# Listing transfers of a batch without pace, and first projections on their own loads, in an attention and mixture-of-experts kernel

## Chip, cores and metric

The kernel runs on one core of a Trainium2 chip. The metric is the device time of one execution in microseconds (us). Engines are named as the profile does: PE (TensorE), ACT (ScalarE), DVE (VectorE), POOL (GpSimd) and SP (SyncE, which here only issues DMAs).

## What is computed

```python
def reference(x, Wq, bq, ..., router_w0, wg0, wu0, wd0, ...):   # x: 8 x 1024 x 256, 16 heads of 16
    x = layernorm(x + attention(x))        # rotary q, k; softmax(q k / 4) v; output projection
    x = layernorm(x + moe(x))
    return x

def moe(x2):                               # all 8192 tokens; two groups g of 32 experts
    scores = softmax(x2 @ router_w[g])
    weight, expert = top_k(scores, 2)
    # token rows sorted by expert, silu(xs @ wg) * (xs @ wu) @ wd, times weight, added back
```

## The kernel before, in words

The program has two phases, `attention_phase` and `expert_phase`. The change lies in the first. It runs one loop over steps t, from -56 to 597, written out for each engine. A batch b has 64 steps, 64b to 64b+63; a unit u is 4 of the 16 heads, 16 steps long. In a step t PE does four things, in order: score tiles of step t+26 (`score`, line 694, into `ps_a`; DVE takes the row maxima of them, line 939), the transposed scores of step t (`score_t`, line 684, into `ps_b`; ACT makes exponentials, line 570), the product with v of step t-2 (`pv`, line 712, 8 matmul records a step, into `ps_o`), and the jobs that `schedule` has put at t: Q and K (`features`, line 625, a quarter of a projection each), V (`values`, line 632), M (the maxima of a unit, transposed), O, T, L and R (output projection, transposed activations, router logits, counts). PE is in order: where one of these waits, the rest waits.

In this text "step n of batch b" is counted by `pv`: the stretch from the start of the product of loop step 64b+n to the next. PE issues that product in loop step 64b+n+2, so what the code puts at loop step 33 falls in step 31 of this count.

Every engine is in order, and each has its own list. SP takes the list `turns`, sorted by step and then by a priority number; each transfer in it is preceded by its waits, and SP stands at them. POOL takes `pool_order`, sorted by step. What bears on the change:

- Heads' projections of a batch's half c go through `split`: ACT writes the features (line 540), SP swaps their halves by DMA (`swap`, line 339), POOL rotates (lines 238, 239, 241; DVE does so for the very first half), DVE masks an upper part (line 259), POOL subtracts (line 249), SP writes both parts out (`parts_out`, line 344), and SP loads them as stacks for a unit (`stack`, line 362, 8 DMAs, priority 1). `score` waits for the stack of its unit. For the first unit of batch b+1 the stack stands at turn 64b+33 and is needed from loop step 64b+38 on; `parts_out` stands at +29 and +30, `swap` of the second half at +49 and +51.
- Listing: each token row of the attention's result is written to the rows of its chosen experts. For tile t (0 to 7) of batch b, SP loads the rows into one of two buffers (`stage_in`, line 440, priority 7, turn 64(b+2) + 27 + 4(t - 1.5), after a wait until the tile before in the same buffer has been written); POOL marks them (line 518) and issues four indirect DMAs (`scatter_rows`, line 106), each after a wait until `pv` has reached 64(b+2) + 26 + 4t + n. So the 32 transfers of batch b go one a step, in loop steps 27 to 58 of batch b+2. Batches 0 to 5 are listed beside attention work (of batches 2 to 7), batch 6 after the last step, batch 7 in the expert phase.
- `split_max` (lines 778, 781) is a chore of DVE at loop step 16u - 10, thus in steps 4, 20, 36 and 52 or just after; `split_upper` (line 259) comes 8 and 11 steps after `k_step`, which is -48 and -16 from the batch's start. `top2` (lines 815 to 824) has DVE do 48 short instructions from loop step 64(b+1)+55 on. `bias_y` is POOL's at +57.
- Start: SP issues the load of x (`s_xt`) and nine parameter loads (`s_par`). PE waits for four memsets of POOL (the ones, line 485, is the last) and for DVE's constants before anything; `features` of batch 0 waits for all nine loads too, as ACT does. V of batch 0 stands at steps -7 to 0, the second Q and K at -24 to -17.

Of the kernel before, what the change touches and what calls it, by code (L numbers as in the profile page):

```python
# [17 lines left out]
SPB = UPB * STEPS  # L18
# [35 lines left out]
def schedule(nb):  # L54
# [3 lines left out]
    for b in range(nb):  # L58
# [3 lines left out]
        for c, at in enumerate((start - 56, start - 24)):  # L62
            for q in range(QUARTERS):
                put(b_jobs, at + q, "Q", b, c, q)
                put(b_jobs, at + QUARTERS + q, "K", b, c, q)
        for i in range(KC):
            put(b_jobs, start - 7 + i, "V", b, i)
# [11 lines left out]
SPILL = 3 * P  # L79
LISTS = NG * TOPK  # L80
# [28 lines left out]
def attention_phase(nc, nb, dram, keep, cols):  # L109
# [25 lines left out]
    with ExitStack() as ctx:  # L135
# [67 lines left out]
        s_list = keep["s_list"]  # L203
        block = ctx.enter_context(nc.Block())
# [6 lines left out]
        k_step = lambda b, c: SPB * b + (-48, -16)[c]  # L211
        pool_order = []
        for b in range(nb):
# [6 lines left out]
            if b < nb - 1:  # L220
                for t in range(KC):
                    pool_order.append((SPB * (b + 2) + 27 + 4 * t, "list", (b, t)))
# [101 lines left out]
        def _(sp):  # L324
            sp.dma_start(x_t[:, :, :], dram["x_t"][0]).then_inc(s_xt, 16)
            for dst, src in ((w_q, "w_q"), (bias, "bias"), (w_k, "w_k"), (consts, "consts"), (trig, "trig"), (w_v, "w_v"),
                             (w_o, "w_o"), (bo_row, "bo_row"), (router, "router")):
# [19 lines left out]
            def stack(u):  # L347
# [6 lines left out]
                sp.wait_ge(s_ones, 2 * NSTK)  # L354
# [91 lines left out]
            for b in range(nb):  # L446
# [13 lines left out]
                if b + 1 < nb:  # L460
                    turns.append((SPB * b + 3, 6, next_x, (b + 1,)))
                    for t in range(KC):
                        turns.append((SPB * (b + 2) + 27 + LISTS * (t - 1.5), 7, stage_in, (b, t)))
# [11 lines left out]
        def _(pool):  # L475

            for i in range(NSTK):
                for n, lo in enumerate((SIDE // 2, SIDE + SIDE // 2)):
                    pool.memset(k_stack[i][lo:lo + SIDE // 2, :, :], -1.0).then_inc(s_ones, 1)
            pool.wait_ge(s_ones, 2 * NSTK)  # L480
            pool.memset(v_sb[0][:, :], 1.0).then_inc(s_ones, 1)
# [7 lines left out]
            pool.wait_ge(s_par, 16 * 9)  # L489
            for _, name, args in pool_order:  # L490
# [19 lines left out]
                elif name == "list":  # L510
# [9 lines left out]
                    for n, (g, kk) in enumerate((g, kk) for g in range(NG) for kk in range(TOPK)):  # L520
                        pool.wait_ge(s_pv, min(SPB * (b + 2) + 26 + LISTS * t + n, n_steps))
# [4 lines left out]
        def _(act):  # L526
# [7 lines left out]
            def features(which, b, c, q):  # L534
                src = arrived()
                if (b, c) == (0, 0):
                    act.wait_ge(s_par, 16 * 9)
# [5 lines left out]
            def values(b, i):  # L543
                src = arrived()
                if b >= 2:
                    act.wait_ge(s_pv, SPB * (b - 1))
                act.activation(v_sb[b % 2][:, i * H * VW:(i + 1) * H * VW].rearrange("p (h d) -> p h d", d=VW)[:, :, 0:DH],
# [53 lines left out]
        def _(pe):  # L601
# [16 lines left out]
            def features(which, b, c, q):  # L618
                out = b_tile()
                if b == 0:  # L620
                    pe.wait_ge(s_par, 16 * 9)
                pe.wait_ge(s_xt, 16 * (b + 1))
# [6 lines left out]
            def values(b, i):  # L629
                out = b_tile()  # L630
                for dc in range(DC):
# [84 lines left out]
            pe.wait_ge(s_ones, 2 * NSTK + 3)  # L716
            pe.wait_ge(s_set, NSET)
            for t in range(first, steps_end):
                ta = t + LEAD
# [29 lines left out]
        def _(vec):  # L749
# [165 lines left out]
            vec.wait_ge(s_par, 16 * 9)  # L915
# [656 lines left out]
```

## Time and profile before

| what | value |
|---|---|
| median of 3 runs | 2739.4 us (2738.84 to 2759.41) |
| the profiled execution's own time | 2749.05 us |
| its span, first to last instruction | 2747.2 us |
| granted TensorE clock, mean over the span | 0.907 |
| first `score` | at 58.5 us |
| first `score_t` (step 0) | at 127.2 us |
| last product with v | at 1845 us |
| expert phase | from 1959.6 us |

All durations come from the profiled execution. A window A:B is in us from its first instruction. In a window restricted to line 712, 8 records (x8) are one step, so a stretch of 24 records is three steps; its length against that of the same steps of another batch tells what was lost in it.

### The profile page before, as it was taken

The numbers are of one execution on the slowest core, as the hardware profiler recorded it, in microseconds if no ns is written. First come the engines' busy times: TensorE is split into PE (matmuls) and PEld (weight loads), VectorE is DVE, ScalarE is ACT, GpSimd is POOL, SyncE is SP. The second block draws the span as 40 slices with busy tenths as digits, with TensorE's granted clock in tenths as the row PEclk, the third lists the DMA queues.
The fourth block names the chain that finished last, engine by engine and source line by source line (L and its number), as shares of the span: only waits on it lengthen the run. The fifth ranks groups of instructions, "written<-read, shape, count | busy, mean of one in ns | idle before, by whom it ended". The sixth has DMA issues, their size and how long they took to land. (4 is left out here: it accounts for less than half of the span.)

```text
span 2747.2 us, 44206 instructions
## 1 busy us (share of the span) xinstructions
PE 2283.7 (83%) x12531; PEld 1149.5 (42%) x12531; DVE 1877.7 (68%) x3693; ACT 1526.6 (56%) x3206; POOL 1090.0 (40%) x963
## 2 busy tenths in 40 slices
PE   2999999999999999999999989983059998999900
PEld 1433333433433433433433333322037776777700
DVE  2988878888779778788778879512315544666766
ACT  0277777767676766766767757750013333333344
POOL 2221230343443444444335342325445554555543
PEclk7899999999999999999989989965579999999955
DMA  4423432533444444443543542223466645788782
GB/s 124 107 44 87 126 79 66 128 83 109 143 105 113 131 111 120 132 123 90 145 124 76 141 130 58 73 65 111 156 228 208 230 148 170 229 238 245 233 293 88
DMA packets 205593, 371.48 MB, mean 135 GB/s; under 512 B 31984, under 2 KB 145136, under 8 KB 201136
## 3 DMA queue, kind: packets, MB, share of 16 engines
q1 hardware_dynamic: 142864, 259.69, 34.7%
q0 software_dynamic: 27552, 75.40, 7.7%
q10 hardware_dynamic: 34944, 33.56, 4.1%
q8 instruction: 112, 1.84, 0.3%
q14 instruction: 121, 0.99, 0.1%
HBM read 206.62 MB, written 135.69 MB: 125 GB/s over the span
## 5 line engine op out<-in xcount | busy, mean ns | idle before, releaser
L939 DVE TENSOR_REDUCE maxima_sb<-ps_a 128x1 f32<-128x1024 f32 x1024 | 1227.1, 1219 | 311.8 <-PE ps_a L694 301.8
L570 ACT ACTIVATE probs_sb<-ps_b 128x512 f32<-128x512 f32 x2048 | 1093.6, 599 | 432.4 <-PE ps_b L684 425.3
L694 PE MATMUL ps_a<-k_stack_sb,q_stack_sb 48*128 48x512 f32 x2048 | 747.9, 457 | 110.9 <-DVE maxima_sb L939 66.6
L684 PE MATMUL ps_b<-q_stack_sb,k_stack_sb 50*128 50x512 f32 x2048 | 789.3, 466 | 12.7 <-issue 7.1
L694 PEld LDWEIGHTS ps_a<-k_stack_sb,q_stack_sb 48*128 48x128 f32 x2048 | 317.5, 192 | 712.3 <-DVE maxima_sb L939 379.6
L712 PE MATMUL ps_o<-probs_sb,v_sb_sb 128*32 128x512 f32 x4096 | 571.0, 631 | 12.7 <-ACT o_raw_sb L578 11.9
L1217 POOL DMA_INDIRECT y_dram<-y_rows_sb,spot_sb x318 | 304.9, 959 | 293.5 <-DVE y_rows_sb L1469 283.4
L684 PEld LDWEIGHTS ps_b<-q_stack_sb,k_stack_sb 50*128 50x128 f32 x2048 | 325.9, 190 | 111.2 <-ACT probs_sb L570 72.6
L1321 PE MATMUL ps_g<-w_gu_sb,x_cols_sb 128*128 x1272 | 357.5, 404 | 6.1 <-issue 2.9
L106 POOL DMA_INDIRECT rows_dram<-stage_sb,listed_sb x224 | 216.6, 967 | 335.9 <-PE ps_o L712 307.1
L1249 ACT ACTIVATE x_cols_sb<-ps_x 128x256 f32<-128x256 f32 x318 | 121.9, 383 | 255.9 <-issue 125.4
L1454 DVE TENSOR_TENSOR spot_sb<-x_rows_sb,spare_sb 128x1 int32<-128x1 int32 x318 | 50.7, 160 | 298.6 <-ACT gate_sb L1269 204.2
L1321 PEld LDWEIGHTS ps_g<-w_gu_sb,x_cols_sb 128*128 128x128 f32 x1272 | 219.2, 192 | 59.0 <-issue 29.6
L238 POOL TENSOR_TENSOR feat_qk_sb<-feat_qk_sb,trig_sb 128x1024 f32<-128x1024 f32 x30 | 71.2, 2374 | 354.9 <-DMA swapped_sb<-feat_qk_sb 267.2
L1269 ACT ACTIVATE gate_sb<-ps_g 128x128 f32<-128x128 f32 x318 | 88.2, 277 | 217.8 <-PE ps_g L1321 165.1
L1339 PE MATMUL ps_y<-w_d_sb,hidden_t_sb 128*128 x636 | 192.7, 385 | 0.0
L1310 PE MATMUL ps_x<-consts_sb,x_rows_sb 128*128 128x128 f32 x636 | 124.1, 278 | 62.8 <-DMA x_rows_sb<-rows_dram 62.8
L712 PEld LDWEIGHTS ps_o<-probs_sb,v_sb_sb 128*32 128x32 f32 x4096 | 83.0, 110 | 184.7 <-ACT probs_sb L570 62.9
L1469 DVE COPY y_rows_sb<-ps_y 128x256 f32<-128x256 f32 x318 | 132.0, 415 | 5.4 <-remote 3.1
L1310 PEld LDWEIGHTS ps_x<-consts_sb,x_rows_sb 128*128 128x128 f32 x636 | 90.3, 143 | 98.1 <-DMA x_rows_sb<-rows_dram 65.9
L540 ACT ACTIVATE feat_qk_sb<-ps_b,bias_sb 128x256 f32<-128x256 f32 x128 | 60.6, 474 | 86.6 <-PE ps_b L625 84.4
L1339 PEld LDWEIGHTS ps_y<-w_d_sb,hidden_t_sb 128*128 128x128 f32 x636 | 97.0, 193 | 25.1 <-issue 1.5
(158 smaller groups left out, 2071.2 us busy)
## 6 DMA issues: line engine op xcount, KB each, us to landing
x_rows_sb<-rows_dram SPq DMA_DIRECT2D x318, 128.5 KB
swapped_sb<-feat_qk_sb SPq DMA_DIRECT2D x64, 256.0 KB
parts_dram<-parts_q_sb SPq DMA_DIRECT2D x16, 1024.0 KB
parts_dram<-parts_k_sb SPq DMA_DIRECT2D x16, 1024.0 KB
q_stack_sb<-parts_dram SPq DMA_DIRECT2D x64, 256.0 KB
k_stack_sb<-parts_dram SPq DMA_DIRECT2D x64, 256.0 KB
w_gu_sb<-w_gu SPq DMA_DIRECT2D x8, 2048.0 KB, 20.2
back_sb<-y_dram ACTq DMA_DIRECT2D x64, 256.0 KB
```

Of the source, the lines that this page charges most:

```text
L106: return pool.indirect_dma_start(dram["rows"][g], bass.IndirectOffsetOnAxis(ap=index, axis=0), source, None)
L570: act.activation(probs[t % NPR][:, j, :], src[:, :], ACT.Exp, scale=float(DH) ** -0.5).then_inc(s_bdrain, 1)
L684: pe.matmul(out[:, :], k_stack[u % NSTK][lo:lo + XROWS, jj, kc * P:(kc + 1) * P].bitcast(F32R), q_stack[u % NSTK][lo:lo + XROWS, jj, qh * ...
L694: ins = pe.matmul(out[:, kh, :], q_stack[u % NSTK][lo:lo + ROWS, jj, qt * P:(qt + 1) * P].bitcast(F32R), k_stack[u % NSTK][lo:lo + ROWS, j ...
L712: ins = pe.matmul(ps_o[32 * j:32 * j + 32, :], v[:, at:at + 32], probs[t % NPR][:, j, :], start=kc == 0, stop=kc == KC - 1)
L939: vec.tensor_reduce(maxima[u % 2][:, 1 - k, i:i + 1], src[:, :, :].rearrange("p a q -> p (a q)"), AX.X, ALU.max).then_inc(s_adrain, 1)
L1217: pool.indirect_dma_start(dram["y"][n // NT], bass.IndirectOffsetOnAxis(ap=spot[n % NSP][:, :], axis=0), y_rows[n % NY][:, :], None).then_ ...
L1249: act.activation(x_cols[n % NXT][:, :, :], ps_x[n % 2][:, 0:DC, :], ACT.Copy).then_inc(s_xc, 1)
L1310: ins = pe.transpose(ps_x[n % 2][:, dc, :], x_rows[n % NXG][:, dc * P:(dc + 1) * P], con("ident"))
L1321: ins = pe.matmul(ps_g[n % 2][:, 0:2 * HID], x_cols[n % NXT][:, dc, :], w_gu[g][:, bass.ds(e * (DC * 2 * HID) + dc * 2 * HID, 2 * HID)], s ...
L1339: pe.matmul(ps_y[n % 2][:, 0:D], hidden_t[n % 2][:, :], w_d[:, bass.ds(e * D + down_at(g), D)], start=True, stop=True).then_inc(s_down, 1)
L1469: vec.tensor_copy(y_rows[m % NY][:, :], ps_y[m % 2][:, 0:D]).then_inc(s_yr, 1)
```

## The change

It makes four edits, all in `attention_phase` and `schedule`.

1. Listing: the first transfer of a batch waits until `pv` has done 64(b+2)+31 steps, the other 31 wait for no step. `pool_order` has tile t at +31+2t (before +27+4t), and `stage_in` stands at turn +31+2(t-1.5), which is 28, 30, 32, ... 42 (before 21, 25, 29, ... 49).
2. The loads of w_q, bias and w_k count on x's semaphore, and the first projections (PE and ACT) wait for those four loads only. The trigonometric table is loaded ahead of the constants. The other waits count six parameter loads.
3. POOL fills the first v buffer before the stacks' rows; PE waits for the memsets and DVE's constants only at step -26. V waits for its own.
4. For batch 0, V moves from steps -7 to 0 to steps -46 to -39, and the second Q and K from -24 to -36 (with them `k_step`, so the swap, the masks and `parts_out` of the half come 12 steps earlier).

```diff
-        for c, at in enumerate((start - 56, start - 24)):
+        for c, at in enumerate((start - 56, start - (36 if b == 0 else 24))):
...
-            put(b_jobs, start - 7 + i, "V", b, i)
+            put(b_jobs, start + i - (46 if b == 0 else 7), "V", b, i)
...
+LIST_AT, LIST_PACE = 31, 2
...
+        x_in = lambda b: 16 * (3 + b + 1)
...
-        k_step = lambda b, c: SPB * b + (-48, -16)[c]
+        k_step = lambda b, c: SPB * b - (48, 28 if b == 0 else 16)[c]
...
-                    pool_order.append((SPB * (b + 2) + 27 + 4 * t, "list", (b, t)))
+                    pool_order.append((SPB * (b + 2) + LIST_AT + LISTS // LIST_PACE * t, "list", (b, t)))
...
-            for dst, src in ((w_q, "w_q"), (bias, "bias"), (w_k, "w_k"), (consts, "consts"), (trig, "trig"), (w_v, "w_v"),
-                             (w_o, "w_o"), (bo_row, "bo_row"), (router, "router")):
+            for dst, src in ((w_q, "w_q"), (bias, "bias"), (w_k, "w_k")):
+                sp.dma_start(dst[:], dram[src][:]).then_inc(s_xt, 16)
+            for dst, src in ((trig, "trig"), (consts, "consts"), (w_v, "w_v"), (w_o, "w_o"), (bo_row, "bo_row"),
+                             (router, "router")):
...
-                        turns.append((SPB * (b + 2) + 27 + LISTS * (t - 1.5), 7, stage_in, (b, t)))
+                        turns.append((SPB * (b + 2) + LIST_AT + LISTS // LIST_PACE * (t - 1.5), 7, stage_in, (b, t)))
...
+            pool.memset(v_sb[0][:, :], 1.0).then_inc(s_ones, 1)
+            pool.wait_ge(s_ones, 1)
             for i in range(NSTK):
...
-                        pool.wait_ge(s_pv, min(SPB * (b + 2) + 26 + LISTS * t + n, n_steps))
+                        if t == n == 0:
+                            pool.wait_ge(s_pv, min(SPB * (b + 2) + LIST_AT, n_steps))
...
                 if (b, c) == (0, 0):
-                    act.wait_ge(s_par, 16 * 9)
+                    act.wait_ge(s_xt, x_in(0))
...
-                if b == 0:
-                    pe.wait_ge(s_par, 16 * 9)
-                pe.wait_ge(s_xt, 16 * (b + 1))
+                pe.wait_ge(s_xt, x_in(b))
...
-            pe.wait_ge(s_ones, 2 * NSTK + 3)
-            pe.wait_ge(s_set, NSET)
             for t in range(first, steps_end):
+                if t == -LEAD:
+                    pe.wait_ge(s_ones, 2 * NSTK + 3)
+                    pe.wait_ge(s_set, NSET)
```

## Rows read from the trace of the kernel before

**Rows 1.** The page's first part: busy time of the engines.

```profile
PE 2283.7 (83%) x12531; PEld 1149.5 (42%) x12531; DVE 1877.7 (68%) x3693; ACT 1526.6 (56%) x3206; POOL 1090.0 (40%) x963
```

**Rows 2.** Windows, line 712 alone: stretch, us, PE busy (x), clock, DMA. Batches 1, 2.

```profile
329.10:541.81 212.71, 70.45 (x512) 0.98 0.38 91
541.81:770.44 228.63, 72.53 (x512) 0.94 0.43 113
```

**Rows 3.** Windows, line 712: steps 60 to 62, batches 1, 2; sum of 1 to 6.

```profile
528.40:538.55 10.15, 3.19 (x24) 1.00 0.38 77
750.27:767.19 16.92, 4.07 (x24) 0.80 0.61 145
...
sum 91.87, PE 23.52; mean PE 3.92
```

**Rows 4.** Windows, line 712: steps 53 to 56, batches 1 to 3; sum of 1 to 6.

```profile
502.16:518.25 16.09, 5.66 (x32) 0.79 0.04 15
720.27:740.12 19.85, 6.00 (x32) 0.74 0.14 49
942.78:955.29 12.51, 4.26 (x32) 1.00 0.26 96
...
sum 103.71, PE 33.38; mean PE 5.56
```

**Rows 5.** Timeline of POOL and DVE in step 53 of batch 2.

```profile
720.52 2.36 POOL L238 TENSOR_TENSOR feat_qk_sb<-feat_qk_sb,trig_sb 128x1024 f32<-128x1024 f32 x1 [8.23 <-DMA swapped_sb<-feat_qk_sb]
...
720.62 2.31 DVE L778 TENSOR_SCALAR max_parts_sb<-maxima_sb 128x32 int32<-128x32 int32 x1
```

**Rows 6.** Start: SP issue, DMA issues (last: us to landing), timeline of PE.

```profile
2.11 0.64 SPq L328 DMA_DIRECT2D w_k_sb<-w_k  x1
...
w_k_sb<-w_k SPq DMA_DIRECT2D x1, 256.0 KB, 5.3
...
16.09 6.51 PE L625 MATMUL ps_b<-x_t_sb,w_q_sb 128*128 128x256 f32 x16 [16.09 <-POOL ones_bf_sb L485]
22.44 3.62 PE L625 MATMUL ps_b<-x_t_sb,w_k_sb 128*128 128x256 f32 x16
58.52 1.23 PE L694 MATMUL ps_a<-k_stack_sb,q_stack_sb 48*128 48x512 f32 x4 [32.47 <-DMA k_stack_sb<-parts_dram]
...
127.18 0.50 PE L684 MATMUL ps_b<-q_stack_sb,k_stack_sb 50*128 50x512 f32 x1
```

**Rows 7.** Timeline of POOL, SP and PE in steps 30 to 35 of batch 2.

```profile
646.48 0.96 POOL L106 DMA_INDIRECT rows_dram<-stage_sb,listed_sb  x1 [1.48 <-PE ps_o L712]
...
650.17 1.73 SPq L362 DMA_DIRECT2D q_stack_sb<-parts_dram  x4
651.94 1.84 SPq L362 DMA_DIRECT2D k_stack_sb<-parts_dram  x4
...
661.74 0.46 PE L694 MATMUL ps_a<-k_stack_sb,q_stack_sb 48*128 48x512 f32 x1 [0.96 <-DMA k_stack_sb<-parts_dram]
```

**Rows 8.** Windows, line 712: steps 35 to 39 of batches 1 and 2.

```profile
440.94:456.96 16.02, 5.33 (x40) 1.00 0.00 0
659.00:675.07 16.07, 5.33 (x40) 1.00 0.43 123
```

**Rows 9.** Timeline of POOL, SP, PE and DVE after the last step (unpaced listing).

```profile
1884.25 1.05 POOL L106 DMA_INDIRECT rows_dram<-stage_sb,listed_sb  x1 [0.55 <-POOL stage_sb L518]
...
1888.14 0.96 POOL L106 DMA_INDIRECT rows_dram<-stage_sb,listed_sb  x1 [0.30 <-issue]
...
1890.78 22.18 SPq L440 DMA_DIRECT2D stage_sb<-x_dram  x5
...
1905.15 1.37 PE L664 MATMUL ps_a<-router_sb,parts_q_sb 128*128 128x64 f32 x8
...
1912.59 0.29 DVE L765 COPY logits_sb<-ps_a 128x128 f32<-128x128 f32 x1 [14.24 <-remote]
...
1929.05 0.96 POOL L106 DMA_INDIRECT rows_dram<-stage_sb,listed_sb  x1 [0.30 <-issue]
```

More of the change, by code:

```diff
@@ L353, in stack @@
                     sp.wait_ge(s_bfill, b_no[("S", STEPS * (u - NSTK + 1) - 1, HEADS[-1])] + 1)
-                sp.wait_ge(s_ones, 2 * NSTK)
+                sp.wait_ge(s_ones, 2 * NSTK + 1)
                 for stk, which, runs in ((q_stack, 0, Q_RUNS), (k_stack, 1, K_RUNS)):
@@ L479, in _ @@
                     pool.memset(k_stack[i][lo:lo + SIDE // 2, :, :], -1.0).then_inc(s_ones, 1)
-            pool.wait_ge(s_ones, 2 * NSTK)
-            pool.memset(v_sb[0][:, :], 1.0).then_inc(s_ones, 1)
             pool.wait_ge(s_ones, 2 * NSTK + 1)
@@ L488, in _ @@
             pool.wait_ge(s_ones, 2 * NSTK + 4)
-            pool.wait_ge(s_par, 16 * 9)
+            pool.wait_ge(s_par, 16 * 6)
             for _, name, args in pool_order:
@@ L546, in values @@
                     act.wait_ge(s_pv, SPB * (b - 1))
+                elif i == 0:
+                    act.wait_ge(s_ones, (1, 2 * NSTK + 2)[b])
                 act.activation(v_sb[b % 2][:, i * H * VW:(i + 1) * H * VW].rearrange("p (h d) -> p h d", d=VW)[:, :, 0:DH],
@@ L630, in values @@
                 out = b_tile()
+                if b == 0:
+                    pe.wait_ge(s_par, 16 * 6)
+                    pe.wait_ge(s_xt, x_in(0))
                 for dc in range(DC):
@@ L913, in between @@
                         room -= cost
-            vec.wait_ge(s_par, 16 * 9)
+            vec.wait_ge(s_par, 16 * 6)
             vec.memset(keep["count"][:, :, :], float(P)).then_inc(s_set, 1)
```

## The prediction, made blind

> **What bounds the kernel now.** I read the page first, for the engines' shares: PE is busy for 83% of the span, DVE for 68%, POOL for 40% [rows 1]. The chain that ended last says little here, since the change lies in the attention phase, and there PE is in order and fed by DVE, ACT and SP at every step. So the question is not how busy POOL is, but at which steps PE loses time, and whether POOL's or SP's listing is behind it. For that I compared the same steps of different batches, in windows restricted to the product with v. Batch 1 has no listing beside it and takes 212.7 us; batch 2 has one and takes 228.6 us, with the same matmuls [rows 2]. Three places differ.
>
> Steps 60 to 62: 10.15 us in batch 1, 16.92 us in batch 2, and the granted clock falls from 1.00 to 0.80 there, so part of the stretch ran at 1.2 GHz. Over batches 2 to 6 the sum is 91.87 - 10.15 = 81.7 us, against 5 x 10.15 = 50.8 [rows 3]: 31.0 us lost. In the timeline eight indirect transfers stand back to back just ahead of it: POOL was held by the split of the next batch from step 48 on, and the last two tiles came late and in a run.
>
> Steps 53 to 56: 12.51 us in batch 3, the best; batches 2 to 6 together 103.71 - 16.09 = 87.6 us, against 5 x 12.51 = 62.6 [rows 4]: 25.1 us lost. Here the cause shows: DVE's short line 778 takes 2.31 us because it began 0.1 us after a tensor operation of POOL of 2.36 us [rows 5]. When POOL's rotation of the second half falls on `split_max`, DVE, and then PE, wait. Batch 1 pays 3.6 us for it without any listing.
>
> The Trainium skill bears on this one: by "SBUF — State Buffer", section "Who interferes with whom", VectorE in a two-port mode and GpSimd take a shared port pair as an exclusive lock, and the later one waits for the whole instruction. By that rule DVE loses the rest of POOL's instruction, whenever the two meet; the trace agrees, with 2.31 us.
>
> Steps 35 to 39: PE waited 0.96 us for the stack of the next batch [rows 7], yet batch 2 took 16.07 us against 16.02 in batch 1 [rows 8]: a wait of a microsecond is absorbed. This load has no slack left.
>
> **Edits 2 to 4, the start.** PE began at 16.09, released by POOL's memset of the ones [rows 6]. After the change it waits for x, w_q, bias and w_k; the last lands at 2.11 + 5.3 = 7.4 [rows 6]. Gain 8.6 us. What follows (projection, swap, DVE's rotation, parts, stack) is a chain of the same lengths up to the first score at 58.52: DVE's constants and the memsets lie beside it. Q ran 6.5 us and K 3.6 us, the slow one first [rows 6]; I keep that order. V and the second Q and K go into PE's wait before 58.5. From there to step 0 it took 127.18 - 58.52 = 68.7 us for 26 steps, 2.64 each, paced by DVE's two reductions; the projections leave these steps, but the clock, which they had raised, then stays at 1.2 GHz until step 0, so I take only 1 us off, and put 2 us back for the first steps with both kinds of scores at the low clock. The swap of the second half and `parts_out` move ahead of stack 1 on SP: about 7 us of slack by my count, so nothing. Start: 8.6 + 1 - 2 = 7.6 us gained. Bounds: 3 (the low clock costs more, or stack 1 is late) and 11.
>
> **Edit 1, what it removes.** With all 32 transfers begun at loop step 33 (step 31 of the count), how long do they take? After the last step the kernel already runs a listing without pace: first transfer at 1884.25, last at 1929.05 [rows 9]: 46 us for 32, a tile being 4 x 1.27 us and the rest waits for its rows. That is 13 to 15 steps, so the run is over before the split at +48. Then steps 60 to 62 look like batch 1's: 31.0 us gained. Bounds: 0, if the loss merely moves with the run, and 31. Steps 53 to 56 should look like batch 1's too, as POOL starts its rotation when the swap lands: 25.1 - 5 x 3.6 = 7.1 us gained. Bounds -10 and 20, by the phase.
>
> **What it adds.** `stage_in` of tile 2 now stands at turn +32, one before the stack of the next batch (+33). It waits until tile 0's transfers have landed, and these now start at loop step 33, not 28. In batch 2: `pv` reaches 31 steps at 646.48. Four transfers take 3 x 1.27 + 0.96 = 4.8 us, to 651.3. Landing takes 1890.78 - (1888.14 + 0.96) = 1.7 us more [rows 9]: 653.0. Issuing the stage load costs 0.4: the stack goes out at 653.4 instead of 650.17. Its eight issues last 3.6 us and its landing was 661.74 [rows 7], 11.6 us from first issue; so 665.0. It shares the queues with eight transfers instead of four and a stage load: 1 us more, 666.0. PE needs it at 661.74 - 0.96 = 660.8. Stall 5.2 us, one absorbed: 4.2 a batch. A stall of that size is followed by low clock (batch 2 lost 19.85 - 12.51 = 7.3 us where lines 778 and 781 of DVE were held some 2.1 us each [rows 4, 5]), so I add 2 us: 6.2 x 5 batches (2 to 6; batch 7 has no successor) = 31 us lost. Bounds: 5 (the stack turns out faster) and 45.
>
> "DMA: Bandwidth & Descriptors" of the Trainium skill, section "Queues, rings and completion order", says that a DMA engine alternates between queues packet by packet; the busier listing would then take up to half of the stack's rate while it lasts, some 3 us instead of my 1, and the added loss would be 41 us. No row here shows the two at that density.
>
> **Late signals in a long run.** In the unpaced run after the last step, PE had finished its router matmul at 1905.15 + 1.37 = 1906.5, and DVE, idle, took it at 1912.59 [rows 9], 6 us late; the first 18 transfers show nothing of the kind. The stall of steps 60 to 62 is of the same make after eight. So the run may carry its own loss into steps 31 to 45. Bounds: 0, and 6 x 6.3 = 38 us at one such stall a batch; more if it grows as in rows 9. I take 0, since the 48 short instructions of `top2` and the write of the parts, which stood beside the eight, are not there; the upper end stays in the range.
>
> **Sum.** -7.6 - 31.0 - 7.1 + 31 = -14.7 us against the profiled 2749.05 us (span 2747.2, 1.9 us around it): 2734.4. That execution is 9.65 us above the median of the runs; taken off the median, 2739.4 - 14.7 = 2725 us. The expert phase is only shifted.
>
> **Rivals.**
> - A, the run is free: the stack lands in time or its stall is absorbed (loss 5, not 31), steps 60 to 62 and the start are gained: -7.6 - 31 - 7 + 5 = -41, 2699 us. For it: the load takes 11.6 us in rows 7 while the DMA queues are full of other things, and might be quicker. Against: SP is in order, and the issue after 653 us is forced by the code.
> - B, slower: late signals. Semaphore updates of PE, ACT and DVE are delayed while POOL issues transfer after transfer, at the steps where each of them waits for the other every microsecond. One stall of 6.3 us per batch gives back what steps 60 to 62 lose; it decides when each batch has more than two. At three a batch in six batches, +113: -7.6 - 31 - 7 + 31 + 113 = +98, 2838 us; at 1.5 a batch +42, 2781 us. For it: rows 9. Against: 18 transfers there went without.
> - C, the losses only move (one stall of 6.3 us in batches 2 to 6, stack stall as summed): -14.7 + 31 = +16, 2756 us.
> - D, the skips seen at steps 60 to 62 belong to the profiled execution. It is 9.65 us longer than the median, so at most a third of the 31 us: -5, 2735 us.
>
> **Chances.** Forecast with its near variants, D among them (2712 to 2740): 40%. A: 29%. C: 16%. B: 15%. The likeliest one's own range is 2705 to 2745. The range for 8 in 10 takes in most of A and the lighter half of B: 2692 to 2790. A measurement of this kernel tells about 1% from no change, that is 27 us: faster by more 33% (A and the edge of the forecast), within 1% 49%, slower by more 18% (B and a part of C).
>
> **What would show it.** Right: first projection near 7.5 us and first score near 50; the swap waits of SP unchanged; in batches 2 to 6 a PE wait for `k_stack` of 3 to 6 us around step 35, followed by a few us at 1.2 GHz, steps 35 to 39 near 22 us; steps 60 to 62 at 10.2 us; 32 transfers within some 50 us from step 31. Wrong: no PE wait at step 35 (then A), or PE, DVE and ACT idle with the release unexplained inside steps 31 to 45 (then B or C), or DVE's line 778 above 2 us in most batches.

## The result, and the profile after

The changed kernel takes 2866.23 us (median of 4 runs, 2857.45 to 2873.4), the kernel before in the same comparison 2739.12 us (4 runs, 2732.05 to 2759.41): a ratio of 1.0448, 95% interval 1.0392 to 1.0504. It is 4.5% slower, where 2725 us in a range of 2692 to 2790 was forecast. The profiled execution took 2863.12 us; its span is 2861.2 us, 114.0 us longer than before. Medians here are over all runs of a kernel and ratios over its undisturbed ones, so a ratio can differ from the quotient of two medians.

The page of after: its first part, and of its fifth the main group of each engine. Below them the same groups of before.

```profile
PE 2358.4 (82%) x12531; PEld 1178.0 (41%) x12531; DVE 1875.0 (66%) x3693; ACT 1532.3 (54%) x3206; POOL 1093.0 (38%) x963
...
L948 DVE TENSOR_REDUCE maxima_sb<-ps_a 128x1 f32<-128x1024 f32 x1024 | 1229.3, 1220 | 400.9 <-PE ps_a L702 302.7
L577 ACT ACTIVATE probs_sb<-ps_b 128x512 f32<-128x512 f32 x2048 | 1097.7, 598 | 561.3 <-PE ps_b L692 464.9
L692 PE MATMUL ps_b<-q_stack_sb,k_stack_sb 50*128 50x512 f32 x2048 | 816.0, 483 | 61.6 <-issue 47.6
```

```profile
L939 DVE TENSOR_REDUCE maxima_sb<-ps_a 128x1 f32<-128x1024 f32 x1024 | 1227.1, 1219 | 311.8 <-PE ps_a L694 301.8
L570 ACT ACTIVATE probs_sb<-ps_b 128x512 f32<-128x512 f32 x2048 | 1093.6, 599 | 432.4 <-PE ps_b L684 425.3
L684 PE MATMUL ps_b<-q_stack_sb,k_stack_sb 50*128 50x512 f32 x2048 | 789.3, 466 | 12.7 <-issue 7.1
```

The work is the same [rows 1], and DVE's and ACT's instructions are as long as they were (1220 against 1219 ns, 598 against 599). The idle time ahead of them is what grew: 89 us more on DVE, 129 us on ACT, and PE's 12.7 us ahead of the transposed scores have become 61.6.

Where this happens is seen in windows restricted to the product with v. Steps 27 to 39 of batches 2, 4, 5 and 7 in after (stretch, us, busy, clock, DMA share, GB/s), the sum over batches 2 to 7, and the same sum and batches 2 and 7 in before:

```profile
625.04:686.07 61.03, 17.33 (x105) 0.76 0.45 132
...
1089.11:1153.23 64.12, 15.91 (x104) 0.83 0.46 133
1324.84:1379.47 54.63, 17.32 (x104) 0.79 0.52 150
...
1781.64:1850.92 69.28, 19.07 (x105) 0.66 0.24 77
sum 371.92, PE 105.10; mean PE 17.52
```

```profile
635.85:675.12 39.27, 13.84 (x104) 1.00 0.53 145
...
1731.10:1768.01 36.91, 13.85 (x104) 1.00 0.23 76
sum 234.06, PE 83.10; mean PE 13.85
```

137.9 us are lost here, against 31 forecast. The DMA share is no higher than before (0.45 against 0.53 in batch 2), and PE's waits for the stack come to 5.2 us in the whole stretch from 600 to 1840 us: waiting for bytes is a small part of it. The other places did what was forecast, or better. Windows of after: steps 60 to 62 of batch 2 and the sum of 2 to 6 (81.7 us in before [rows 3]), then steps 53 to 56 of batch 2 and that sum (87.6 in before [rows 4]).

```profile
755.52:765.67 10.15, 3.19 (x24) 1.00 0.38 73
...
sum 50.75, PE 15.98; mean PE 3.20
```

```profile
731.78:745.37 13.59, 4.26 (x32) 1.00 0.05 17
...
sum 69.64, PE 22.17; mean PE 4.43
```

The start, in the timeline of after (first projection, first score, first product with v), answers to rows 6:

```profile
7.77 5.47 PE L630 MATMUL ps_b<-x_t_sb,w_q_sb 128*128 128x256 f32 x16 [7.77 <-DMA w_k_sb<-w_k]
13.07 3.62 PE L630 MATMUL ps_b<-x_t_sb,w_k_sb 128*128 128x256 f32 x16
...
49.41 1.22 PE L702 MATMUL ps_a<-k_stack_sb,q_stack_sb 48*128 48x512 f32 x4 [8.83 <-DMA k_stack_sb<-parts_dram]
...
124.31 1.08 PE L720 MATMUL ps_o<-probs_sb,v_sb_sb 128*32 128x512 f32 x4
```

What fills the 137.9 us is seen in the timeline of batch 2. It answers to rows 9.

```profile
673.39 0.39 PE L702 MATMUL ps_a<-k_stack_sb,q_stack_sb 48*128 48x512 f32 x1
...
675.38 0.97 POOL L107 DMA_INDIRECT rows_dram<-stage_sb,listed_sb  x1 [0.28 <-issue]
...
676.58 0.30 PE L656 MATMUL ps_b<-consts_sb,max_parts_sb 128*64 128x128 f32 x1 [1.61 <-issue]
676.65 0.96 POOL L107 DMA_INDIRECT rows_dram<-stage_sb,listed_sb  x1 [0.30 <-issue]
677.92 0.96 POOL L107 DMA_INDIRECT rows_dram<-stage_sb,listed_sb  x1 [0.30 <-issue]
679.18 0.96 POOL L107 DMA_INDIRECT rows_dram<-stage_sb,listed_sb  x1 [0.30 <-issue]
682.26 1.08 ACT L577 ACTIVATE probs_sb<-ps_b 128x512 f32<-128x512 f32 x2 [5.74 <-remote]
682.30 1.23 DVE L948 TENSOR_REDUCE maxima_sb<-ps_a 128x1 f32<-128x1024 f32 x1 [7.21 <-remote]
...
682.91 2.07 PE L630 MATMUL ps_b<-x_t_sb,w_q_sb 128*128 128x256 f32 x4 [6.04 <-ACT probs_sb L577]
```

PE's last matmul ends at 676.88; then PE, ACT and DVE all stand, each waiting for another, while only POOL issues, and they move again 2 us after POOL's last transfer. In batch 7 they also move again at 1807.0, while POOL is still issuing. That it is the signal that comes late can be read from the trace: the scores that DVE waited for were done at 673.39 + 0.39 = 673.78, and the semaphore update that released it is recorded at 682.27. The waits of DVE and ACT in after between 600 and 1840 us (total, times, longest):

```profile
DVE maxima_sb L948 <- remote: 81.9, 20, 10.7
...
ACT probs_sb L577 <- remote: 67.7, 21, 9.3
```

"Remote" is a wait that ended with a semaphore update ahead of which the profile shows no work that had just ended; for "issue" it shows no such update at all. In the same window of before DVE's line has 1.0 us of "remote" and 7.9 of "issue" (in after 15.0), ACT's none and 2.3. Below, "late signals" means these waits.

### The profile page after: what moved, and what is told of

The parts are those of the page before. It is cut to its first block and busy times, and to the rows that moved or that the text cites. A ratio compares the mean times of both kernels' runs of the same rounds, so it can differ in the third digit from the quotient of the medians.

```text
span 2861.2 us, 44164 instructions
## 1 busy us (share of the span) xinstructions
PE 2358.4 (82%) x12531; PEld 1178.0 (41%) x12531; DVE 1875.0 (66%) x3693; ACT 1532.3 (54%) x3206; POOL 1093.0 (38%) x963
## 5 line engine op out<-in xcount | busy, mean ns | idle before, releaser
L948 DVE TENSOR_REDUCE maxima_sb<-ps_a 128x1 f32<-128x1024 f32 x1024 | 1229.3, 1220 | 400.9 <-PE ps_a L702 302.7
L692 PE MATMUL ps_b<-q_stack_sb,k_stack_sb 50*128 50x512 f32 x2048 | 816.0, 483 | 61.6 <-issue 47.6
L702 PE MATMUL ps_a<-k_stack_sb,q_stack_sb 48*128 48x512 f32 x2048 | 773.5, 470 | 88.4 <-DVE maxima_sb L948 64.8
L702 PEld LDWEIGHTS ps_a<-k_stack_sb,q_stack_sb 48*128 48x128 f32 x2048 | 329.8, 198 | 709.2 <-DVE maxima_sb L948 378.0
L720 PE MATMUL ps_o<-probs_sb,v_sb_sb 128*32 128x512 f32 x4096 | 597.1, 657 | 12.5 <-ACT o_raw_sb L585 10.3
L692 PEld LDWEIGHTS ps_b<-q_stack_sb,k_stack_sb 50*128 50x128 f32 x2048 | 337.6, 198 | 183.1 <-issue 94.2
L1330 PEld LDWEIGHTS ps_g<-w_gu_sb,x_cols_sb 128*128 128x128 f32 x1272 | 219.6, 192 | 58.3 <-issue 25.9
L630 PE MATMUL ps_b<-x_t_sb,w_q_sb 128*128 128x256 f32 x256 | 81.1, 448 | 27.9 <-ACT probs_sb L577 10.6
## 6 DMA issues: line engine op xcount, KB each, us to landing
w_gu_sb<-w_gu SPq DMA_DIRECT2D x8, 2048.0 KB, 19.3
```

Of the source, the lines that this page charges most:

```text
L692: pe.matmul(out[:, :], k_stack[u % NSTK][lo:lo + XROWS, jj, kc * P:(kc + 1) * P].bitcast(F32R), q_stack[u % NSTK][lo:lo + XROWS, jj, qh * ...
L702: ins = pe.matmul(out[:, kh, :], q_stack[u % NSTK][lo:lo + ROWS, jj, qt * P:(qt + 1) * P].bitcast(F32R), k_stack[u % NSTK][lo:lo + ROWS, j ...
L720: ins = pe.matmul(ps_o[32 * j:32 * j + 32, :], v[:, at:at + 32], probs[t % NPR][:, j, :], start=kc == 0, stop=kc == KC - 1)
L948: vec.tensor_reduce(maxima[u % 2][:, 1 - k, i:i + 1], src[:, :, :].rearrange("p a q -> p (a q)"), AX.X, ALU.max).then_inc(s_adrain, 1)
L1330: ins = pe.matmul(ps_g[n % 2][:, 0:2 * HID], x_cols[n % NXT][:, dc, :], w_gu[g][:, bass.ds(e * (DC * 2 * HID) + dc * 2 * HID, 2 * HID)], s ...
```

## The experiments

The runs were made in sets, each on one chip. The table shows where eleven profiled executions stand against the span of before, stretch by stretch (differences of windows, us; "rest" is batches 0 and 1 and the other steps of 2 to 6). The chip of each is named where it is known, since the set turned out to matter. One profiled execution stands for each kernel, and it need not be a typical one: that of after_last1 is the slowest of its ten runs, that of one_then_two_2 among the fastest of its twelve.

| kernel (chip) | start | rest | 27-39, b2-6 | 40-52 | 53-56 | 60-62 | batch 7 | after the last step | sum |
|---|---|---|---|---|---|---|---|---|---|
| after | -8.3 | -3.4 | +105.5 | +5.8 | -18.0 | -31.0 | +58.2 | +5.2 | +114.0 |
| list_only (13) | +0.2 | -12.1 | +101.1 | +14.7 | -10.3 | -31.0 | +58.2 | +3.6 | +124.4 |
| start_only (13) | -7.9 | -5.2 | -0.7 | +0.1 | -8.6 | -8.0 | +18.6 | +5.4 | -6.1 |
| stack_first (13) | -7.2 | -1.7 | +108.5 | +6.5 | -16.8 | -31.0 | +60.6 | +2.2 | +121.2 |
| pace2 (13) | -8.8 | -7.1 | +44.6 | 0.0 | -19.6 | -31.0 | +31.5 | +2.7 | +12.4 |
| pace2_stack (2) | -7.3 | -11.0 | +27.4 | 0.0 | -15.6 | -31.0 | +31.3 | +6.2 | +0.1 |
| burst4 (3) | -9.0 | -5.6 | +41.4 | +4.0 | -4.5 | -31.0 | +34.4 | +4.0 | +33.7 |
| pace2_last1 (3) | -8.4 | -2.6 | +28.9 | 0.0 | -17.4 | -31.0 | 0.0 | +1.2 | -29.4 |
| after_last1 (8) | -7.4 | -2.3 | +41.9 | +0.1 | -19.3 | -31.0 | +25.9 | -10.8 | -2.9 |
| after_last1_2 (2) | -7.6 | -7.6 | +103.5 | +11.4 | -14.1 | -31.0 | -4.2 | +7.2 | +57.6 |
| one_then_two_2 (9) | -8.3 | +0.3 | +7.1 | +1.7 | -21.0 | -31.0 | -3.9 | +4.0 | -51.0 |

**Which of the two halves: start_only and list_only.** The first is after with the listing of before:

```diff
-pool_order.append((SPB * (b + 2) + LIST_AT + LISTS // LIST_PACE * t, "list", (b, t)))
+pool_order.append((SPB * (b + 2) + 27 + 4 * t, "list", (b, t)))
...
-                        if t == n == 0:
-                            pool.wait_ge(s_pv, min(SPB * (b + 2) + LIST_AT, n_steps))
+                        pool.wait_ge(s_pv, min(SPB * (b + 2) + 26 + LISTS * t + n, n_steps))
```

> The kernel after with the listing of before (one transfer per step, from step 27 on, stage loads at their old turns); what is left of the change is the start. Theory (the loss is all in the unpaced listing): first product with v near 124.3 us as after, batches 2 to 6 as long as before (215 to 229 us), so about 8 us less than before, 2731 against 2739. Rival (the start edits leave a worse phase or a lower clock behind, as batch 0 with +7 us and its low clock until 127 us hint): 2740 or more.

The second is the same in reverse, applied to before.

> The kernel before with the listing of the change alone. Theory: the changed kernel's time plus the 8 us of the start, 2874; batches 2 to 7 each 7 to 58 us longer than before, almost all of it in steps 27 to 45. Rival (the two parts make it together): under 2850.

Measured: start_only 2745.45 us, ratio 1.0016 (0.9976 to 1.0056); list_only 2881.16, ratio 1.0463 (1.0398 to 1.0528). The whole loss is the listing. The time of start_only came out on its rival's side (2740 us or more), though: the start gains its 8 us (first product with v at 124.8), but in this execution batch 7 gave back 18.6, with the listing of before and no late signal in it. 17.4 of them are in its steps 40 to 52, where the clock is at 0.64:

```profile
1737.83:1795.24 57.41, 19.93 (x105) 0.64 0.27 86
```

**Order on SP, and a tie to PE's steps: stack_first and pace2.** The first moves one stage load behind the next batch's stack, the second ties each transfer to a step, two per step:

```diff
-turns.append((SPB * (b + 2) + LIST_AT + LISTS // LIST_PACE * (t - 1.5), 7, stage_in, (b, t)))
+turns.append((SPB * (b + 2) + LIST_AT + LISTS // LIST_PACE * (t - 1.5) + 1.5 * (t == 2), 7, stage_in, (b, t)))
```

> The changed kernel with the stage load of the third tile turned to stand behind the stack of the next batch instead of ahead of it on SP. Theory (late signals): the stack's stall of 2 to 3.5 us in batches 2 and 3 goes, the gaps without releaser stay, 2850 to 2870. Rival (the stack behind the stage load is what the loss begins with, as the prediction had it): at least 31 us less than after, 2835 or below.

```diff
-                        if t == n == 0:
-                            pool.wait_ge(s_pv, min(SPB * (b + 2) + LIST_AT, n_steps))
+                        pool.wait_ge(s_pv, min(SPB * (b + 2) + LIST_AT + (LISTS * t + n) // LIST_PACE, n_steps))
```

> The changed kernel, but each transfer again waits for a step of its own, two per step from step 31 on: the same transfers, the same 16 steps, the same stage turns. Theory (what hurts is that POOL issues transfer after transfer at 1.27 us spacing): the gaps of 3 to 7 us with no releaser in steps 31 to 45 go, steps 27 to 39 near 45 us instead of 58 to 66, and the time is at most 2740. Rival (position or load: 32 transfers with their stage loads in 16 steps hurt however they are spaced): 2840 or more.

Measured: stack_first 2864.48 us, ratio 1.0393 (1.0329 to 1.0457): nothing gained. The stack is not what the loss begins with. pace2 2764.06 us, ratio 1.0032 (0.9999 to 1.0065), above the 2740 expected, but 100 us better than after for one wait. In batch 2 its 32 transfers begin between 632.5 and 688.5 us, those of after between 636.3 and 693.7: the mean rate is the same. So it is not the mean rate that hurts. I read it so: a tied POOL stops as soon as PE is late, and a stall does not grow. With the late signals mostly gone (DVE has no "remote" left, and 16.9 us of "issue" in 24 waits of at most 1.1), the wait that was forecast comes out, here in PE's waits of pace2:

```profile
PE ps_a L701 <- DMA k_stack_sb<-parts_dram: 26.9, 5, 6.2
```

5.4 us a batch; 5.2 were forecast.

**Both: pace2_stack.** It has the edits of pace2 and stack_first.

> Two transfers per step from step 31 as in pace2, and the stage load of the third tile turned behind the stack. In pace2 PE waited 4.5 to 6.2 us for the stack in each of batches 2 to 6 (the 5.2 us that the prediction had), and steps 35 to 39 took 23.0 to 27.4 us against 16. Theory (that wait is the load behind the stage load on SP): it goes, 7 us x 5 = 35 us less than pace2's 2764, 2729. Rival (the stack is slow because its transfers share the DMA engines with the listing): the wait stays above 3 us and the time within 10 us of pace2.

Measured: 2748.67 us, ratio 1.0011 (0.9972 to 1.0051). PE's wait for the stack is gone from batches 2 to 6, but steps 27 to 39 still lose 27.4 us, with short late signals (PE's "issue" waits come to 18 us) and a clock of 0.92 to 0.96. Of the 35 us expected 15 came by the medians, 17 in these steps, and only 0.2% by the ratios, each taken against before on its own chip.

**What in the transfers delays the signals: half_rows, plain, half_parts.** Their listing writes to tables of its own, so the expert phase reads blank rows for batches 0 to 6 and writes its own rows without indices; its time is left out of the comparison. Each is one execution. In this order, half_rows, half_parts and plain (the closing semaphore counts left out):

```diff
-scatter_rows(pool, rows[:, kk, :], g, kk, listed[:, kk, g, at:at + 1], dram)
+pool.indirect_dma_start(dram["half"][g], bass.IndirectOffsetOnAxis(ap=listed[:, kk, g, at:at + 1], axis=0), rows[:, kk, 0:D // 2], None)
...
+pool.indirect_dma_start(dram["half"][g], bass.IndirectOffsetOnAxis(ap=listed[0:P // 2, kk, g, at:at + 1], axis=0), rows[0:P // 2, kk, :], None)
...
+pool.dma_start(dram["flat"][LISTS * m + n], rows[:, kk, :])
```

> The changed kernel with the 28 x 8 listing transfers of the attention phase made half as wide (128 floats of each row, into a table of their own); the lists that the expert phase reads are blank there, filled by plain transfers at the end of the attention phase, so only the batches are compared, not the whole time. Same number of transfers, rows and indices, half the bytes. If bytes in flight delay the signals: batches 2 to 6 near 215 to 222 us, as before. If it is the number of transfers or of rows: 229 to 235 us, as in after.

> As half_rows, but each listing transfer of the attention phase is a plain one of full width, issued by POOL from the same tile to consecutive rows of a table of its own: same bytes, no indices. If the indices (the way POOL makes the row addresses) delay the signals: batches 2 to 6 near 215 to 222 us. If any dense run of transfers does: 229 us or more. Batch lengths alone are compared.

> As half_rows (batches alone are compared), but each indirect transfer takes 64 rows of full width instead of 128 rows of half: same number of transfers, half the bytes, half the rows and indices. If the number of rows that a run puts out delays the signals: batches 2 to 6 near 215 to 224 us and idle time without releaser far below after's 20 to 60 us a batch. If the number of transfers does: 229 to 236 us as in half_rows.

Measured on chip 2: half_rows has batches 2 to 6 at 230.6 to 235.8 us, plain at 214.8 to 221.0 and batch 7 at 191.9. The waits of DVE's reduction in half_rows (600 to 1840 us); in plain neither DVE nor ACT has any such wait in that window:

```profile
DVE maxima_sb L956 <- remote: 94.5, 17, 10.8
DVE maxima_sb L956 <- issue: 9.8, 11, 2.1
```

Half the bytes change nothing; the same bytes without indices, on the same DMA queue (1536 packets, 4.21 MB in batch 2, as in after), delay nothing. But plain differs in a second thing. Its transfers take POOL 0.54 us each, and the stage loads then hold it up, so in batches 2 and 3 its longest run without a pause is 8 transfers in 5.0 us; in half_rows and after it is 16 in 20.5 us. Whether the indices or the time that POOL issues without a pause make the difference stays open. The timeline of POOL in plain, four transfers in 2.14 us:

```profile
657.62 2.14 POOL L534 DMA_DIRECT2D flat_dram<-stage_sb  x4 [0.30 <-POOL stage_sb L529]
```

half_parts came out at 216.2 to 223.9 us without late signals, but on chip 8, and there the listing of after, with all its rows, showed none either, as after_last1 below tells.

**Breaking the run: serial, pairs_landed, burst4.** All begin at step 31 as after. In serial each transfer waits for the landing of the one before, in pairs_landed each pair for the last pair, and burst4 waits for a step ahead of every fourth (pairs_landed and burst4 have the edit of stack_first too):

```diff
+                        elif n:
+                            pool.wait_ge(s_list[t % 2], 16 * (LISTS * (m // 2) + n))
...
+                        elif n % 2 == 0:
+                            last = m - (n == 0)
+                            pool.wait_ge(s_list[last % 2], 16 * (LISTS * (last // 2) + (n or LISTS)))
...
-                        if t == n == 0:
+                        if n == 0:
+                            pool.wait_ge(s_pv, min(SPB * (b + 2) + LIST_AT + LISTS * t // LIST_PACE, n_steps))
```

> The changed kernel, begun at step 31 and not tied to PE's steps, but each transfer issued only when the one before it has landed: one in flight at a time. Theory (signals are late when several indirect transfers are in flight at once): the gaps of 3 to 7 us without releaser go, batches 2 to 6 each under 222 us, the whole under 2790. Rival (POOL's own issuing or anything else at these steps delays them, whatever is in flight): batches 2 to 6 over 228 us, the whole over 2840.

> The changed kernel, stage load of the third tile behind the stack, transfers not tied to PE's steps but in pairs: the next pair only when the last has landed, about 2 in 4.5 us, 32 in 75 us. Theory (what counts is the length of the run without a pause, not the tie to PE): the idle time without releaser stays under 5 us a batch, as in serial (0 to 1); the listing then ends near step 57 and the next batch's split and stack are late, so the time is near 2850 to 2950 in spite of it. Rival (only the tie to PE helps): gaps of 20 us and more a batch.

> The kernel of pace2_stack with the wait for PE's step kept only ahead of every fourth transfer: four in a row each two steps, the same 32 in 16 steps. Theory (a run of indirect transfers delays the signals, and a wait for PE's step cuts the run as soon as PE is late): four in a row take 5.1 of the 5.8 us of two steps, so the run is cut less soon than in pace2_stack; idle time without releaser of PE, ACT and DVE between the 2 to 5 us a batch of pace2_stack and the 20 to 60 of after, and 2755 to 2800 us. Rival (the spacing within the pair matters, not the cut): as after, 2850.

Measured: serial 3003.47 us, pairs_landed 2829.3, burst4 2781.38 (ratios 1.0916, 1.0287, 1.0105). The time expected of serial was missed by over 200 us, its mechanism was not: steps 27 to 34 take 23.2 us as in before, and idle time without a shown releaser is at most 1.5 us per engine and batch. What it costs is elsewhere, in PE's waits of serial:

```profile
PE ps_a L706 <- DMA k_stack_sb<-parts_dram: 60.5, 10, 11.8
PE ps_b L696 <- DMA q_stack_sb<-max_rows_sb: 57.8, 5, 15.3
```

The listing takes 113 us in batch 2, SP stands at stage loads that wait for it, and the stacks and maxima rows stand behind them. pairs_landed is the same in small: steps 27 to 39 at 39.2 us, at most 3.7 us of short waits per engine and batch, then 75 us lost in steps 40 to 59, and a time below the 2850 to 2950 expected. burst4 lies between pace2_stack and after in time and in steps 27 to 39 (41.4 us lost, against 27.4 and 105.5), as the theory had it. The waits themselves don't show the order so well: gaps of ACT over 0.3 us without a releaser sum to 17.8, 18.9 and 57.2 us over batches 2 to 6 of pace2_stack, burst4 and after. That four in a row cost more than two is thus shown by the time alone, and on two chips.

**The last batch, and a surprise: pace2_last1, after_last1, and after_last1 again.** The listing beside batch 7 is as in before, the rest as in pace2_stack and as in after; the edit of the second:

```diff
+LAST = lambda b, nb: b == nb - 3
...
+                        if LAST(b, nb):
+                            pool.wait_ge(s_pv, SPB * (b + 2) + 26 + LISTS * t + n)
-                        if t == n == 0:
+                        elif t == n == 0:
```

> pace2_stack with the listing beside the last batch as before, one per step from step 27 on. In pace2_stack the last batch took 227.2 us, in before 195.9: short stalls in steps 31 to 37, then the low clock up to the end of it. Theory (the stalls start the low clock, and nothing brings it back in that batch): the last batch is near 196 us again, the whole 30 us less than pace2_stack, 2719. Rival (the clock falls there in some executions whatever the listing does, as start_only with 214.6 us hints): 2735 to 2750.

> The changed kernel with the listing beside the last batch alone as before (one per step from step 27). Theory: what the unpaced run cost there (254.2 against 195.9 us) goes, all else stays: 58 us less than after's 2863, 2805. Rival (the last batch's clock falls for another reason that batches 2 to 6 bring along): over 2830.

Measured: pace2_last1 2723.03 us, ratio 0.9890 (0.9845 to 0.9934), batch 7 at 195.9 us: as expected. after_last1 2727.08 us, ratio 1.0049 (1.0002 to 1.0096), where 2805 was expected: batches 2 to 6 too had lost their late signals, with not a line of their listing changed. The kernel before was fast in that set as well (2719.48 us, against 2739 to 2772 in the others). So the same two kernels ran again:

> The same kernel as after_last1, again. There batches 2 to 6 took 218 to 221 us with not one late signal, though their listing is that of after (229 to 236 us); the kernel before was 30 us faster in that job than in the others, too (2719 against 2739 to 2772), and it was another chip. Theory (the late signals depend on the chip as well): in a job in which before takes 2739 us or more, batches 2 to 6 have 20 us and more of idle time without releaser each, and the time is near 2805. Rival (the listing of the last batch alone decides, also for the batches ahead of it): no late signals here either, and a time within 15 us of before.

> The same kernel as half_parts, again, beside after_last1_2 on one chip. If that one shows the late signals and this does not (batches 2 to 6 at 216 to 224 us), the number of rows of a run of indirect transfers decides; if both show them (229 us and more), the number of transfers. If neither does, it stays open.

Measured on chip 2: after_last1_2 2800.29 us, ratio 1.0127 (1.004 to 1.0214), where before took 2772.21. The waits of DVE and ACT between 600 and 1840 us, and the windows of steps 27 to 39 of batches 2 to 4 with the sum of 2 to 7, on chip 8 (two fences) and on chip 2 (two fences), the same program:

```profile
ACT probs_sb L580 <- issue: 0.6, 1, 0.6
```

```profile
626.84:674.20 47.36, 14.71 (x104) 0.89 0.51 144
845.23:893.06 47.83, 14.72 (x104) 0.89 0.51 142
1063.36:1112.68 49.32, 16.45 (x104) 0.83 0.55 159
...
sum 276.03, PE 90.05; mean PE 15.01
```

```profile
DVE maxima_sb L951 <- remote: 67.1, 15, 8.0
DVE maxima_sb L951 <- issue: 9.1, 11, 1.8
...
ACT probs_sb L580 <- remote: 50.8, 16, 6.7
```

```profile
621.59:675.77 54.18, 15.40 (x104) 0.87 0.52 143
854.72:916.51 61.79, 17.33 (x104) 0.76 0.45 130
1087.72:1152.58 64.86, 18.19 (x104) 0.76 0.45 132
...
sum 337.53, PE 95.93; mean PE 15.99
```

So something outside the program decides whether a run of indirect transfers delays the signals. Chip 8 is in one set only, with no late signal in any of its three profiles, and chip 2 in two sets, with them in both; that it is the chip is the nearest reading, but chip and set are not told apart. half_parts_2, beside after_last1_2 on chip 2, has the late signals in full (batches 2 to 6 at 234.3 to 241.3 us; DVE's "remote" 94.2 us in 18). Halving the bytes, or the rows with them, changes nothing. What was not halved is the number of indirect transfers in a row, and with it POOL's time for them (1.20 us each with 64 rows, 1.27 with 128).

**Versions about 1% faster than before: three_in_two and one_then_two.** The step of transfer i in three_in_two, then in one_then_two, with one per step in the last batch in both:

```diff
+LIST_AT = 27
+list_step = lambda b, i, nb: LIST_AT + (i if b >= nb - 3 else 2 * i // 3)
...
+list_step = lambda b, i, nb: 27 + i if b >= nb - 3 or i < 8 else 31 + i // 2
...
+                        pool.wait_ge(s_pv, min(SPB * (b + 2) + list_step(b, LISTS * t + n, nb), n_steps))
```

> A candidate: three transfers in two steps from step 27 on (done by step 48, ahead of the split), one per step in the last batch, the stage load of the fourth tile behind the stack. Theory: late signals nearly absent (under 2 us a batch), no stack wait above before's 1 us, steps 60 to 62 at 10.2 us: 31 us less than start_only, 2715, last batch near 196. Rival (C of the prediction: the losses only move): 2735 or more.

> A candidate: one transfer per step from step 27 to 34, while the stack of the next batch lands, then two per step up to step 46; one per step in the last batch. Theory: steps 27 to 39 as before (39.2 us, where pace2_last1 took 44 to 47), steps 60 to 62 at 10.2 us: about 20 us less than pace2_last1, 2700. Rival (the two per step cost their 4 to 6 us a batch wherever they stand): 2718 to 2730.

> The same kernel as one_then_two, again. There its profiled execution took 2666.82 us against 2719 of before, without a late signal, on the chip that shows none, and two of its four executions were disturbed. In a job in which before takes 2739 us or more: theory (what pace2_last1 still loses in steps 27 to 39 comes of two transfers per step beside the stack, not of the two per step as such): steps 27 to 39 at 39 to 41 us, late signals under 5 us a batch, 2700, a ratio near 0.98. Rival (two per step cost their 4 to 6 us a batch wherever they stand, on such a chip): steps 40 to 52 at 49 us and more, 2718 to 2730. Where before is near 2719 again, the ratio should be 0.985, with nothing left to lose at steps 60 to 62 but the start and the last batch.

Measured: three_in_two 2726.88 us, ratio 0.9881 (0.9779 to 0.9984), but steps 27 to 39 lose 38.8 us, and the stack wait that was to stay at 1 us is there, in PE's waits:

```profile
PE ps_a L702 <- DMA k_stack_sb<-parts_dram: 17.6, 5, 4.5
```

one_then_two, on chip 8, took 2666.82 us in its profiled run and 2713.14, 5510.59 and 6818.3 us in the others, so no median of it stands. one_then_two_2, on chip 9: 2719.33 us (12 runs) against 2759.88 (17 runs), ratio 0.9902 (0.985 to 0.9955). By its median it missed the 2700 expected and falls in its rival's range; the profiled run, at 2698.31 among the fastest of the twelve (2696.22 to 2734.16), is the one that the steps below are read from. No listing without pace ran on chip 9, so how strongly that chip delays signals is not known; this profile has one "remote" wait of DVE, of 2.4 us. Its windows of steps 27 to 39, batches 2 and 3 and the sum of 2 to 7, against before's 234.06:

```profile
627.47:667.81 40.34, 13.85 (x104) 1.00 0.56 156
838.73:879.03 40.30, 13.85 (x104) 1.00 0.55 156
...
sum 241.16, PE 83.10; mean PE 13.85
```

Steps 40 to 52 lose 1.7 us in five batches at two transfers per step. So, as far as profiles from chips 9, 3 and 2 can be compared, two per step cost little as such (1.4 us a batch in steps 27 to 39 of one_then_two_2), and 5.8 and 5.5 us a batch beside the stack, in pace2_last1 and pace2_stack.

## Why the prediction was wrong

- **Start.** Right: 7.6 us forecast, 8.3 measured (6.1 to 9.0 in the kernels that have it). PE's start at 7.77 was forecast at 7.4, the first score at 49.41 near 50; from there to the first product with v 0.8 us were lost, where the sum had 1.
- **Steps 60 to 62.** Right: 31.0 forecast and measured, in every kernel whose listing ends ahead of the split. start_only, with the old listing, kept 23 of it.
- **Steps 53 to 56.** Right in sign, too small: 7.1 forecast, 18.0 measured. Batch 0, which the sum had left out, gave 7.0 us back, 5.7 of them in its own steps 53 to 56. That part is luck: no listing stands beside batch 0, the kernels with the new start have the same code there, and they took 194.9 to 205.2 us for it.
- **The stack behind `stage_in`.** The mechanism was right, and hidden in after: there PE waited 5.2 us for the stack in all, where that much a batch was forecast, since it was late itself. With the signals in time it shows: 5.4 us a batch in pace2, 6.8 in after_last1 on chip 8, 5.2 forecast. Its price in steps 27 to 39 was undersized: 239.02 - 197.15 = 41.9 us in after_last1 (windows of batches 2 to 6, at a clock of 0.83 to 0.93), 31 forecast. "DMA: Bandwidth & Descriptors" of the Trainium skill, section "Queues, rings and completion order", led to 41; the trace agrees in the size, but no run shows the engines alternating, and the waits alone come to 33.9 us in after_last1, 26.9 in pace2 and 25.0 in plain.
- **Late signals in the long run: the step that failed.** "I take 0, since the 48 short instructions of `top2` and the write of the parts, which stood beside the eight, are not there". The late signals were there all the same: on chip 2 the listing of after costs some 62 us more in steps 27 to 39 of batches 2 to 6 than on chip 8 (103.5 against 41.9), 12 us a batch, with nothing of `top2` near. The bound of 38 us rested on one stall a batch, since the first 18 transfers of rows 9 went without. But after the last step PE, DVE and ACT hand little to each other, and in the attention steps each waits for another about every microsecond; I take that for the reason why the stalls were more here, no run varies it. Of the signs of being wrong, "PE, DVE and ACT idle with the release unexplained" is what came. Rival B named the mechanism and its place, with a chance of 15%: three stalls of 6.3 us a batch, 2838 us. The trace has 20 "remote" waits of DVE in six batches, 3.3 a batch, of 4.1 us each on average; the measured time is 28 us more.
- **Batch 7.** Not in the sum at all: +58.2 us. 32.4 are in steps 27 to 39, from late signals and from the clock, which falls in step 33 and stays low. 24.6 are steps 40 to 52 at that clock, here the window of after, and under it that of before:

```profile
1850.92:1915.53 64.61, 25.14 (x105) 0.50 0.16 50
```

```profile
1768.01:1808.03 40.02, 13.85 (x105) 1.00 0.36 120
```

"No successor" was read as "no loss": there is no stack to be late for, but the listing runs there too. In batches 2 to 6 the clock is back soon: their steps 40 to 52 lose 5.8 us in all. How much of the 24.6 the listing is to blame for stays open, since start_only lost 17.4 us there with the listing of before.

The sum by these terms: -8.3 - 3.4 + 105.5 + 5.8 - 18.0 - 31.0 + 58.2 + 5.2 = +114.0 us. On chip 8, with batch 7 paced, the start (-7.4 us) and steps 60 to 62 (-31.0) came out as forecast, steps 53 to 56 (-19.3 for -7.1) and the stack (+41.9 for +31) larger. Against before on the same chip that kernel was still 0.5% slower, and after itself did not run there.

## What to carry to other kernels

Don't let POOL issue indirect transfers one after another beside engines that hand work to each other every microsecond. Tie each one or two to a step of the engine that must not be late: the mean rate can stay the same (pace2: 102 us less than after by the medians). Where a trace shows one stall of such a make at a place where the engines hand little to each other, don't price it at nothing elsewhere: here it came 3.3 times a batch. Run a kernel more than once before the absence of such stalls is believed, since one set here had none, and put transfers that something waits for (here the next stack) where the run is thinnest.

## What the hardware showed unasked

- Beside indirect transfers of POOL in a row, 1.27 us apart, signals between PE, ACT and DVE come late; the waits are up to 10.7 us long in after. Plain transfers of the same bytes, at 0.54 us each and with longer pauses of POOL between them, show no such wait; half the bytes or half the rows make no difference; pairs of which each waits for the last to land, one in 5.3 us in batch 2 of pairs_landed, delay by 1.7 us at most. The instructions themselves are not longer. The Trainium skill, "SBUF — State Buffer", section "Who interferes with whom", has it that a DMA never contends with a compute engine. For the instructions the trace agrees; the time between them is not covered by that rule.
- It differs between sets of runs, and it seems between chips: none on chip 8, some 60 us on chip 2 with the same program. The kernel before took 2719 us there and 2751 to 2772 on chips 13, 3, 9 and 2 (2713 and 2742 to 2765, as averages of the runs that the ratios go by). The 31 us of its steps 60 to 62 would be about all of the smallest of these differences, but before was not profiled on chip 8. What distinguishes the chips stays open.
- In every profile the clock falls to 1.2 GHz in batch 7, before's included, and but for a few us it stays there to the end of the batch. What differs is the step: 33 in after and list_only, 37 in pace2 and burst4, 39 in after_last1 (with 37.0 us in steps 27 to 39 and no stall), 45 in start_only, 53 in before, 56 in after_last1_2, the same program as after_last1. Where steps 40 to 52 are wholly at the low clock and nothing else holds them, they take 64.6 us instead of 40.0. Late signals go with an early fall, but it comes early without them too, and what starts it stays open. It can be a good part of the 2714 to 2746 us over which the ten runs of after_last1 spread.
